# Attention values packed by the scalar engine for heads 1 to 7, in one buffer with the adjacency words

## What is computed

```python
feats   = einsum('bnf,hfu->bhnu', X, W)
e_self  = einsum('bhnu,hu->bhn', feats, a_self)
e_neigh = einsum('bhnu,hu->bhn', feats, a_neigh)
dense   = leaky_relu(e_self[..., :, None] + e_neigh[..., None, :], 0.2)
att     = softmax(dense + NEG_BIG * (1 - A), axis=-1)
out     = relu(einsum('bhij,bhju->bhiu', att, feats) + b)
x1      = layernorm(x + out)
agg     = einsum('bij,bjf->bif', adj, x1) / max(sum(adj, -1), 1e-6)
y       = layernorm(x1 + relu(einsum('bnf,of->bno', concat[x1, agg], W1)))
```

## Time and profile before

| | |
|---|---|
| median of 3 runs | 3283.79 us (3280.23 to 3284.34) |
| the profiled execution | 3279.78 us, its span 3278.0 us |
| mean granted TensorE clock | 0.997 |
| TensorE busy | 3228.9 us, 99% |
| VectorE busy | 2351.1 us, 72% |
| ScalarE busy | 1866.4 us, 57% |
| GpSimd busy | 284.0 us, 9% |
| a batch | some 202 us, about half of it the heads |

### The profile page before, as it was taken

The page is one execution under the profiler, slowest core; times in us unless marked ns, Lnnn a source line. Parts: engine busy times, 40 slices in busy tenths (PEclk is TensorE's granted clock), DMA queues, the critical chain, the costliest instruction groups (busy, mean ns, idle before and its releaser), DMA issues.

```text
span 3278.0 us, 124485 instructions
## 1 busy us (share of the span) xinstructions
PE 3228.9 (99%) x56896; PEld 2745.0 (84%) x56896; DVE 2351.1 (72%) x4224; ACT 1866.4 (57%) x2456; POOL 284.0 (9%) x251
## 2 busy tenths in 40 slices
PE   7999999999999999999999999999999999999998
PEld 6969789697896978979788797987979879697895
DVE  6858678586785857858578585875858768586685
ACT  4646456474664746647465474664737556465563
POOL 0010200102011020100201002020020200202001
PEclk9999999999999999999999999999999999999999
DMA  7153162421615225252252513425144151431501
GB/s 216 57 114 100 51 158 66 110 97 52 156 62 120 84 60 154 63 130 67 71 145 61 142 55 79 142 58 141 53 100 121 57 146 62 106 110 51 140 30 52
DMA packets 368653, 314.48 MB, mean 96 GB/s; under 512 B 285056, under 2 KB 285056, under 8 KB 368128
## 3 DMA queue, kind: packets, MB, share of 16 engines
q1 hardware_dynamic: 368128, 306.52, 34.2%
HBM read 205.26 MB, written 34.08 MB: 73 GB/s over the span
## 4 chain that ended last, share of the span: by engine, by line
PE 90%; DVE 5%; DMA 3%; ACT 1%; issue 1%; SPq 0%; DVEq 0%; POOL 0%; ACTq 0%
PE six L901 78%; PE pair L901 10%; DVE mask L734 2%; DMA s_bc<-self_scores 1%; DMA self_scores<-sc_row 1%; PE pair L925 1%; PE six L925 1%; DVE rest L644 1%; DVE x_parts L640 1%; ACT step L500 0%; DVE trl L866 0%; ACT trh L465 0%; DMA adj_nat<-in_adj_dram 0%; DVE feat L678 0%; DVE third L646 0%
## 5 line engine op out<-in xcount | busy, mean ns | idle before, releaser
L901 PE MATMUL six<-x_parts,mask 128*128 128x65 bf16 x16384 | 1546.9, 192 | 8.8 <-DVE mask L734 7.6
L901 PEld LDWEIGHTS six<-x_parts,mask 128*128 128x128 fp8e4 x16384 | 1536.0, 97 | 16.5 <-issue 8.2
L901 PE MATMUL six<-third,mask 128*128 128x65 bf16 x16384 | 1546.6, 192 | 2.4 <-issue 2.0
L901 PE MATMUL six<-rest,mask 128*128 128x65 bf16 x16384 | 1546.9, 195 | 1.2 <-issue 1.2
L901 PEld LDWEIGHTS six<-third,mask 128*128 128x128 fp8e4 x16384 | 1536.3, 98 | 4.2 <-issue 4.2
L901 PEld LDWEIGHTS six<-rest,mask 128*128 128x128 fp8e4 x16384 | 1530.9, 96 | 1.5 <-issue 0.8
L500 ACT ACTIVATE step<-s_bc,n_step 128x1024 uint16<-128x1024 f32 x1024 | 1089.3, 1137 | 363.6 <-DVE mask L734 344.0
L734 DVE TENSOR_TENSOR mask<-adj_t,step 128x1024 uint16<-128x1024 uint16 x1024 | 649.9, 685 | 47.6 <-ACT step L500 47.1
L901 PE MATMUL six<-adj_t,x_parts 128*128 128x512 fp8e4 x1536 | 386.4, 380 | 9.8 <-DVE trl L866 5.4
L443 POOL TENSOR_TENSOR s_bc<-feat,rden 128x512 f32<-128x512 f32 x112 | 124.8, 1119 | 2742.2 <-DVE s_bc L779 2728.6
L901 PEld LDWEIGHTS six<-adj_t,x_parts 128*128 128x128 f16 x1536 | 146.2, 98 | 200.1 <-DVE trl L866 13.2
(11 more groups left out here) (125 smaller groups left out, 4560.7 us busy)
## 6 DMA issues: line engine op xcount, KB each, us to landing
s_bc<-self_scores SPq DMA_DIRECT2D x128, 512.0 KB, 3.8
mask<-in_adj_dram SPq DMA_DIRECT2D x64, 512.0 KB, 4.4
adj_nat<-in_adj_dram SPq DMA_DIRECT2D x64, 512.0 KB, 4.3
xs<-in_x_dram SPq DMA_DIRECT2D x128, 256.0 KB, 4.2
out_dram<-mask SPq DMA_DIRECT2D x128, 256.0 KB, 3.4
adj_nat<-in_x_dram SPq DMA_DIRECT2D x64, 256.0 KB, 5.8
step<-in_x_dram SPq DMA_DIRECT2D x64, 256.0 KB, 4.0
xs<-in_L_gnn_W_dram SPq DMA_DIRECT2D x1, 2048.0 KB, 13.3
```

What stands on the lines that cost most here:

```text
L901: return pe.matmul(o, l, r, start=start, stop=stop, skip_group_check=True)
```

## The change

For heads 1 to 7 ScalarE copies the first and the second part out of their 4-byte words into packed rows; head 0 is multiplied from the words as before. The copies of head h stand ahead of the step that is five after the mask at which VectorE makes the values, and each waits for VectorE's instruction that makes its words. TensorE waits at the start of each of these heads for both copies. All three packed parts lie in one buffer, in rows of 66 values, 132 bytes; it also holds the adjacency words of the next batch, in the memory of the first part and a share of the second. The buffers third and adj_word are gone, and wa32 of the set-up lies in key_w.

```diff
+    PACKED_FROM = 1
...
+    VALUES_AT = {(h - 1) * T + (4 if h > 1 else 6): h for h in range(1, H)}
...
-        adj_word = sb("adj_word", [P, WORD_SLOTS, N], U16)
+        ROW_BF = U1 + 1
+        rows_bf = sb("rows_bf", [P, PARTS, 4 * T * ROW_BF], BF16)
+        packed = rows_bf[:, :, :].rearrange(
+            "p r (s k t u) -> p r s k t u", s=2, k=2, t=T)[:, :, :, :, :, 0:U1]
+        adj_word = rows_bf[:, :, :].rearrange("p r n -> p (r n)")[:, 0:WORD_SLOTS * N].bitcast(U16).rearrange(
+            "p (s n) -> p s n", s=WORD_SLOTS)
...
-        third = sb("third", [P, 2, 2, T, ROW], BF16)[:, :, :, :, 0:U1]
-
...
-        val = [(upper_half(val32[i]), upper_half(rest32[i]), third[:, i]) for i in range(2)]
+        val = [(upper_half(val32[i]), upper_half(rest32[i]), packed[:, 2, i]) for i in range(2)]
...
-        wa32 = sb("wa32", [P, KC, SC], F32)
+        wa32 = key_w[:, 0].rearrange("p t h -> p (t h)").rearrange("p (c n) -> p c n", c=KC)
...
+        val_packed = signal("val_packed", 2 * (H - PACKED_FROM))
...
+                def pack_values(h):
+                    for part, made in enumerate((val_f32, val_rest)):
+                        act.wait_ge(made.sem, made.at(b, h + 2))
+                        copy(packed[:, part, h % 2], val[h % 2][part]).then_inc(val_packed.sem, 1)
+
...
                 for g in range(H * T):
+                    if g - STEP_SLOTS - 1 in VALUES_AT and VALUES_AT[g - STEP_SLOTS - 1] >= PACKED_FROM:
+                        pack_values(VALUES_AT[g - STEP_SLOTS - 1])
                     make_step(g)
...
-                    if jt == (4 if h else 6) and h < H - 1:
-                        value_parts(b, h + 1)
+                    if g in VALUES_AT:
+                        value_parts(b, VALUES_AT[g])
...
                     sides = (high_bytes(words), low_bytes(words))
+                    parts = val[h % 2]
+                    if h >= PACKED_FROM:
+                        parts = [packed[:, part, h % 2] for part in range(PARTS)]
...
-                                         val[h % 2][part][:, kind, jt, :],
+                                         parts[part][:, kind, jt, :],
...
                     pe.wait_ge(val_p2.sem, val_p2.at(b, h + 2 if h else 1))
+                    if h >= PACKED_FROM:
+                        pe.wait_ge(val_packed.sem, val_packed.at(b, 2 * (h - PACKED_FROM + 1)))
```

## The result

The changed kernel takes 3261.8 us (median of 4 runs, 3259.6 to 3263.7) where the kernel before took 3282.0 in the same runs: a ratio of 0.9938, 95% interval 0.9921 to 0.9955, some 20 us faster. The forecast was 67 us. The time lies within the range given, but the gain is less than a third of what was foretold. The profiled execution has a span of 3259.7 us, 18.3 less than before.

A forecast was written before the change was run, and what follows sets the result against it. TensorE, busy for 99% of the span, was taken to bound the kernel; 69 us from packing less 2 us for a mask wait gave 67 off 3279.8, 3213, or 3217 as median of runs; range 3194 to 3270 us.

The forecast's parts named there:

- the three differences: TensorE's mean gaps between neighbouring starts of 65-column matmuls, first, second, third part: 29.9, 33.1, 30.7 ns; forecast nearly equal after packing.
- the new wait: TensorE's semaphore wait for ScalarE's copies at the start of heads 1 to 7: never holds, taken as 0, at most 3 us.
- rows off a multiple of 16: Rival, chance 0.07: TensorE pays for 132-byte rows beginning inside a 16-byte block; 3293 us, or 3318 if every row paid.
- copies so slow that ScalarE is the bound: Rival, chance 0.05: ScalarE's copies take 1.65 us each, 11.75 us in a head; at most 22 us gained, 3262 us.
- the main term: Packed parts on TensorE, heads 1 to 7: 1.6 ns less for each of 43008 matmuls, 69 us gained.
- I take 29.6, between 29.3 and 29.9: Forecast time in ns of one 65-column matmul on TensorE in heads 1 to 7 after packing, against 31.2 before.
- The first rival: Smaller price of the stride, from the ratio of two 512-column matmul rows: 30.2 ns, 43 us less 2, 3243 us; chance 0.22.
- The bound of 29.3: Fastest packed pace for TensorE's 65-column matmuls: 27.1 ns of columns plus 2.2 from a 512-column row; 82 us gained.
- the smallest of the three mean differences: 29.9 ns, TensorE's mean gap from first to second part's start; used as upper end for the packed pace.
- the order of three: Start gaps on TensorE differing by part (29.9, 33.1, 30.7 ns), taken as evidence that the moving operand's stride limits the pace.
- five faster tiles arrive 0.38 us earlier: TensorE reaches head 3's sixth mask earlier and waits some 0.1 us for VectorE, once in a batch: 2 us lost.
- hidden by an order that exists already: Rows of 132 bytes and the buffer shared with the adjacency words: no new wait needed, cost 0.

## Why the prediction came out too high

**Right.** TensorE bounds the heads, and packing makes it faster; the three differences became equal; the copies cost 1.08 us (1.06 foretold) and lie in ScalarE's wait with 0.80 us to spare (0.8 foretold); VectorE's wait for TensorE in an ordinary head is 0.92 us (about 0.7 foretold for a larger gain); the new wait never held TensorE in the changed kernel; the shared buffer brought no wait; rows off a multiple of 16 brought no loss against rows of 144 bytes. That the time fell within the range is luck in part: its upper end was drawn from copies so slow that ScalarE is the bound, which didn't come, and the 13 us below stood in no rival.

**Wrong, 28 of the 67 us: the size of the main term.** The step "I take 29.6, between 29.3 and 29.9". It measured 30.25, a gain of 0.96 ns instead of 1.6, 41 us instead of 69. The first rival, the ratio of the two 512-column rows on two parts of three, gave 30.2 and 1.0 ns and hit the number; that was luck. Its 226.7 ns belongs to float32 matmuls in which nothing is read at a stride, and with their weights at the other place the same row takes 233.3; the same sum, 2/3 x 0.085 x 29.3, then gives 1.7 ns and 29.5. And the ladder shows no price that goes by the share of strided parts. The rest of the excess isn't the moving operand's stride: with all three parts packed, and two of three weight loads side by side too, 30.24 ns remain; what they consist of is open. The bound of 29.3 came from carrying a row of 512 columns to 65.

And the smallest of the three mean differences was no sign of a packed matmul's own time. It was misread a little: 29.9, 33.1 and 30.7 ns come from starts rounded to 10 ns, to the nanosecond they are 30.1, 32.8 and 30.7. Above all, differences within a triple shift among neighbours, as the kernel with one strided part shows, and only their sum is the pace.

What I drew from the order of three, that the limit lies in the moving operand, did hold. By the Trainium skill, "SBUF — State Buffer", Specifications, two hits on a 16-byte line are enough for the full rate, and a value every 4 bytes has four. The measurement decides against it for this read: three parts read in this way take 31.93 ns and packed ones 30.24. The same entry says that each cross to a new line costs, and a strided row crosses more of them; no run here tells that from the stride itself.

**Wrong, 8 us: "five faster tiles arrive 0.38 us earlier".** The margin of head 3's sixth mask was read rightly, 0.3 to 0.5 us. But I counted TensorE's gain from the start of head 3, as if VectorE were tied to it there by the sums. The row that would have told is VectorE's first on the sums that head 3 waits for, in the kernel before:

```profile
1111.13 0.56 DVE L662 TENSOR_TENSOR x_parts<-six,qry_w 128x390 f32<-128x390 f32 x1
```

It bears no wait. VectorE runs free from head 0 on (46.0 us from its first mask to head 3's sixth in both kernels), so 21 tiles count, and with 1.0 us of gain the wait is 0.7 us, not 0.1: 10 us instead of 2.

**Wrong, 13 us: a term that wasn't in the sum.** I costed the shared buffer and the shorter rows at nothing, "hidden by an order that exists already". Order was all I looked at. The buffer grew, and everything allocated behind it moved; two operands of matmuls that the change doesn't touch came to a worse place. Moved back, they gave 11.7 us of it. The trace of before had a hint that such a thing exists, float32 matmuls of one form that differ by their buffers:

```profile
L901 PE MATMUL six<-w0h,trh 128*128 128x512 f32 x448 | 178.2, 398 | 2.4 <-DVE w1l L629 2.4
...
L901 PE MATMUL six<-w1h,x1t_l 128*128 128x512 f32 x256 | 99.8, 390 | 0.0
```

But no row gives the price of a move.

Together: 69 - 41 is 28 too much for the pace, 8 for the wait, 13 for the places; 67 - 28 - 8 - 13 = 18 us, the difference of the two spans.

## What to carry to other kernels

When one engine gets faster, don't count its gain from the last place where another engine stands near it, but from the last place where that engine really waited for it; in between the whole gain is spent against the margin. A new or longer buffer is an edit to every buffer behind it: compare the groups of the instructions that the diff doesn't touch first, and try the buffer at the end of the order before giving up on the change. A difference between neighbours' starts tells that operands matter, the length of an unbroken piece over its count how much, to some 0.1 ns; for less than that, take the time from head to head over all batches.

## What the chip showed that was not expected

- A float32 matmul of 512 columns takes 226.7 or 233 ns, by where its weights lie: 640 or 1024 modulo 2048 bytes, with its moving operand in place. 384 unused bytes move a kernel by 10 to 13 us.
- 65 packed bfloat16 columns take 30.24 ns in rows of 132 bytes, 30.46 in rows of 144 and 30.51 in rows of 130; the rows' length moves other buffers too, and which of the two counts is open.
- With one, two and three of three parts at every fourth byte: 30.96, 31.2, 31.93 ns. One strided part costs nearly as much as two. What rule gives this ladder is open.
- Weights at every second byte, or two loads of three side by side: 30.24 ns either way.
